# A chunked recurrence: new rows' store and sums' load move from SyncE to GpSimd, and gram blocks are spread by ScalarE

## What is computed

```python
def step(St, inp):
    kt, qt, vt, at, bt = inp
    Sk = jnp.einsum('bhij,bhj->bhi', St, kt)
    err = Sk - vt
    Sn = at[..., None] * St - (bt[..., None] * err)[..., None] * kt[:, :, None, :]
    ot = jnp.einsum('bhij,bhj->bhi', Sn, qt)
    return (Sn, ot)
```

## Time and profile before

| | us |
|---|---|
| median of 3 runs | 3041.19 |
| lowest, highest | 3038.26, 3052.78 |
| the profiled execution | 3051.64 |
| its span | 3050.0 |
| recurrence, first copy at L595 to the last output bank | 681.6 to 1915.7 |

### The profile page before, as it was taken

How to read it: one execution, slowest core, us unless ns; L and a number is a source line. 1 busy time by engine, 2 the same in 40 slices (tenths; PEclk the granted TensorE clock), 3 DMA queues, 4 the chain that set the end, 5 groups by cost and what they waited for, 6 DMA issues and landing times. The chain is left out here.

```text
span 3050.0 us, 41308 instructions
## 1 busy us (share of the span) xinstructions
PE 2080.3 (68%) x12114; PEld 1426.5 (47%) x12114; DVE 1852.3 (61%) x4462; ACT 1056.3 (35%) x2356; POOL 1183.0 (39%) x1443
## 2 busy tenths in 40 slices
PE   8999999966766666556556446599967553479700
PEld 4555555534555554444345335578733331157600
DVE  5777777767776677776667548545537482023234
ACT  2555555534444444444334234222300100112200
POOL 1444444446443333333333323244444217311175
PEclk8999999987787787787777777799989565579955
DMA  3666666663677788999999993422221602048732
GB/s 93 121 121 121 120 121 121 121 148 71 155 189 176 198 210 222 232 243 240 245 241 251 263 281 82 155 76 76 77 83 33 218 11 71 1 144 264 219 101 84
DMA packets 680751, 457.64 MB, mean 150 GB/s; under 512 B 309583, under 2 KB 625790, under 8 KB 674312
## 3 DMA queue, kind: packets, MB, share of 16 engines
q1 hardware_dynamic: 550891, 314.96, 40.9%
q0 software_dynamic: 50080, 96.70, 11.8%
q10 hardware_dynamic: 79616, 44.06, 5.0%
HBM read 245.54 MB, written 207.77 MB: 149 GB/s over the span
## 5 line engine op out<-in xcount | busy, mean ns | idle before, releaser
L918 ACT ACTIVATE p_diag_o<-p_ident,p_gd 128x128 f32<-128x128 f32 x1152 | 361.7, 389 | 509.2 <-PE p_ps_o L874 483.2
L384 DVE SCALAR_TENSOR_TENSOR p_y<-p_ps_proj,p_w,p_y 128x508 f32<-128x508 f32 (+2 forms) x576 | 416.0, 741 | 115.4 <-ACT p_y L298 101.8
L874 PE MATMUL p_ps_o<-p_ws,p_diag_o 128*128 128x128 f32 x1792 | 327.3, 340 | 128.4 <-DVE p_ws L620 80.0
L726 POOL DMA_DIRECT2D p_near_g<-gram x512 | 284.5, 565 | 289.3 <-PE p_ps_n L847 288.8
L874 PEld LDWEIGHTS p_ps_o<-p_ws,p_diag_o 128*128 128x128 f32 x1792 | 284.0, 240 | 200.6 <-DVE p_ws L620 101.8
L833 PE MATMUL p_ps_z<-p_turned,p_gcol 112*32 112x128 f32 x3584 | 159.6, 319 | 318.3 <-DMA p_turned<-history 318.2
L234 PE MATMUL p_ps_proj<-p_x,p_w 128*128 128x512 f32 x768 | 343.1, 597 | 2.7 <-ACT p_beta_t L289 2.7
L198 POOL TENSOR_TENSOR p_kq<-p_y,p_sig 128x512 f32<-128x512 f32 x128 | 162.2, 1271 | 377.6 <-ACT p_sig L309 376.9
L833 PEld LDWEIGHTS p_ps_z<-p_turned,p_gcol 112*32 112x32 f32 x3584 | 104.7, 126 | 382.4 <-DMA p_turned<-history 343.0
L570 DVE SCALAR_TENSOR_TENSOR p_zo<-p_ws,p_gd,p_zo 128x128 f32<-128x128 f32 x768 | 243.9, 351 | 3.8
L564 DVE TENSOR_TENSOR p_ws<-p_ws,p_dec 128x128 f32<-128x128 f32 (+2 forms) x192 | 119.0, 620 | 205.7 <-PE p_ps_o L874 205.7
(11 more groups left out here) (223 smaller groups left out, 3837.0 us busy)
## 6 DMA issues: line engine op xcount, KB each, us to landing
history<-p_hist SPq DMA_DIRECT2D x18, 2048.0 KB, 14.9
gram<-p_gram SPq DMA_DIRECT2D x64, 512.0 KB, 5.4
history_sums<-p_sums ACTq DMA_DIRECT2D x112, 256.0 KB, 5.5
p_zo<-history_sums SPq DMA_DIRECT2D x28, 1024.0 KB, 8.3
p_wgu<-in_wguT SPq DMA_DIRECT2D x64, 352.0 KB
decays<-p_dec SPq DMA_DIRECT2D x64, 256.0 KB, 2.3
beta_v<-p_bv SPq DMA_DIRECT2D x64, 256.0 KB, 2.5
p_dec<-decays POOLq DMA_DIRECT2D x32, 512.0 KB, 6.5
```

The lines of the kernel that those rows point to most:

```text
L384: nc.vector.scalar_tensor_tensor(out=yv[:, :, s:], in0=pv[:, :, 0:T - s], scalar=par[j % 2][:, kind, TAPS - 1 - s:TAPS - s], in1=yv[:, :, ...
L726: pool.dma_start(near_g[h * HALF:(h + 1) * HALF, :, f, h, :], gram_dram[g * BG:(g + 1) * BG, c, c * C:c * C + HALF, h, e0:e0 + HALF] .rear ...
L874: nc.tensor.matmul(ps_o[s // 4 % 2][:, s % 4, :], diag_o[p // DO % NDO][:, p % DO, :], rows[:, r, :], start=(s % 4 == 0 and r == 0), stop= ...
L918: last = nc.scalar.activation(diag_o[n % NDO][:, p % DO, :], ident[:], ACT.Copy, scale=gd[g][:, r, s:s + 1])
```

## The change

- The two stores of a leaf's new rows are issued by GpSimd (`store_u`) right after its wait for leaf_done, ahead of the decays' second half. SyncE waits only for their landing.
- The two loads of the history sums are issued by GpSimd (`load_sums`), for leaf at - 1 in leaf at, behind `load_near(at + 1)` and ahead of the wait for leaf_done.
- `store_o(at)` comes in leaf at, behind leaf_done, in place of the next leaf's beginning.
- `load_near` loads the gram columns compact, 8 DMAs a leaf of 128 rows by 32 values, into part of `near_t` (`near_c`). It waits until near_turn's second half of the leaf before has read near_t (`x_done`), not only for the near products.
- ScalarE (`near_blocks`) makes near_g of it in 16 activations of 128 x 128, each scaled by a column of `own_head`, which is 1 where the partition belongs to head h and 0 elsewhere. It does so behind step 11 (HALF + 3) of the leaf before, and for leaf 0 ahead of everything. near_g is no longer cleared.
- At the start GpSimd issues load_near(0) ahead of the clears and makes own_head; `cleared` comes behind all of it.

```diff
--- before.py
+++ after.py
@@ -437,6 +437,7 @@
     NW = 2
     BANKS = 4
     CHAINS = 4
+    CLEARED = 5 + 2 * NTURN
     UNITS_AFTER = (0, 0, 1, 2, 2, 2, 3, 3)
     UNITS_NEAR = UNITS - sum(UNITS_AFTER)
     with ExitStack() as ctx:
@@ -456,7 +457,9 @@
         diag_o = [m.sb(f"p2_diag_o{i}", [P, DO, P]) for i in range(NDO)]
         near_w = m.sb("p2_near_w", [P, BG, DH])
         near_g = m.sb("p2_near_g", [P, BG, 2, H, HALF])
+        own_head = m.sb("p2_own_head", [P, H])
         near_t = m.sb("p2_near_t", [DH, BG, H, HALF])
+        near_c = near_t[:].rearrange("p b h e -> p (b h e)")[:, 0:BG * 2 * C].rearrange("p (b s) -> p b s", b=BG)
         ps_z = [m.ps(f"p2_ps_z{i}", [P, UB * QUADS, DH]) for i in range(NZ)]
         NN = 2
         ps_n = [m.ps(f"p2_ps_n{i}", [DH, BG // 2, H * HALF]) for i in range(NN)]
@@ -473,7 +476,8 @@
         half_done = m.sem("p2_half_done")
         leaf_done = m.sem("p2_leaf_done")
         near_in = [m.sem(f"p2_near_in{i}") for i in range(2)]
-        near_g_in = m.sem("p2_near_g_in")
+        near_c_in = m.sem("p2_near_c_in")
+        near_g_made = m.sem("p2_near_g_made")
         near_mm = m.sem("p2_near_mm")
         near_cp = m.sem("p2_near_cp")
         x_done = m.sem("p2_x_done")
@@ -718,39 +722,63 @@
             def load_near(at):
 
                 c, g = divmod(at, GR)
-                if at:
-                    pool.wait_ge(near_mm, at * BANKS)
-                for h in range(H):
-                    for f in range(2):
-                        e0 = f * C + HALF
-                        pool.dma_start(near_g[h * HALF:(h + 1) * HALF, :, f, h, :],
-                                       gram_dram[g * BG:(g + 1) * BG, c, c * C:c * C + HALF, h, e0:e0 + HALF]
-                                       .rearrange("b r e -> r b e")).then_inc(near_g_in, DMA)
+                pool.wait_ge(x_done, at * BANKS)
+                for b in range(BG):
+                    pool.dma_start(near_c[:, b, :], gram_dram[g * BG + b, c, c * C:c * C + HALF]
+                                   .rearrange("r h e -> h r e")).then_inc(near_c_in, DMA)
+
+            def load_sums(at):
+
+                c, g = divmod(at, GR)
+                pool.wait_ge(o_out[g], (c + 1) * DMA)
+                if c + 1 < ROUNDS:
+                    pool.wait_ge(kept[g], (c + 1) * 2)
+                for half in range(2):
+                    seqs = slice(half * ZB * H, (half + 1) * ZB * H)
+                    for i in range(NS):
+                        pool.wait_ge(z_out[i], (at * (BG // NS) + (half + 1) * (ZB // NS)) * DMA)
+                    pool.dma_start(zo[g][seqs].rearrange("p f s i -> p (f s) i"), sums_dram[g, seqs]).then_inc(zo_in[g], DMA)
+
+            def store_u(at):
+
+                c, g = divmod(at, GR)
+                for half, rows in ((0, zo[g][:, 0, 1:1 + HALF, :]), (1, w[g][:, 1 + HALF:, :])):
+                    r0 = c * C + half * HALF
+                    pool.dma_start(hist_dram[g, r0:r0 + HALF].rearrange("r p i -> p r i"), rows).then_inc(u_saved[g], DMA)
 
             load_half(0, 0)
             load_gram(0, 0)
             load_half(0, 1)
             load_gram(0, 1)
+            load_near(0)
+            nc.gpsimd.memset(ident[:], 0.0).then_inc(cleared, 1)
+            nc.gpsimd.memset(own_head[:], 1.0).then_inc(cleared, 1)
+            pool.wait_ge(cleared, 2)
+            nc.gpsimd.affine_select(out=ident[:], in_=ident[:], compare_op=ALU.not_equal, fill=1.0, base=0,
+                                    pattern=[[-1, P]], channel_multiplier=1).then_inc(cleared, 1)
+            nc.gpsimd.affine_select(out=own_head[:], in_=own_head[:], compare_op=ALU.is_ge, fill=0.0, base=0,
+                                    pattern=[[-HALF, H]], channel_multiplier=1).then_inc(cleared, 1)
+            pool.wait_ge(cleared, 4)
+            nc.gpsimd.affine_select(out=own_head[:], in_=own_head[:], compare_op=ALU.is_ge, fill=0.0, base=HALF - 1,
+                                    pattern=[[HALF, H]], channel_multiplier=-1).then_inc(cleared, 1)
             for i in range(NTURN):
                 nc.gpsimd.memset(turned[i][:], 0.0).then_inc(cleared, 1)
                 nc.gpsimd.memset(gcol[i][:], 0.0).then_inc(cleared, 1)
-            nc.gpsimd.memset(near_g[:], 0.0).then_inc(cleared, 1)
-            nc.gpsimd.memset(ident[:], 0.0).then_inc(cleared, 1)
-            pool.wait_ge(cleared, 2 * NTURN + 2)
-            nc.gpsimd.affine_select(out=ident[:], in_=ident[:], compare_op=ALU.not_equal, fill=1.0, base=0,
-                                    pattern=[[-1, P]], channel_multiplier=1).then_inc(cleared, 1)
-            pool.wait_ge(cleared, 2 * NTURN + 3)
-            load_near(0)
+            pool.wait_ge(cleared, CLEARED)
             for at in range(LEAVES):
                 c, g = divmod(at, GR)
-                if at:
-                    store_o(at - 1)
                 send_rows(at)
                 if at + 1 < LEAVES:
                     load_half(at + 1, 0)
                     load_near(at + 1)
-                    pool.wait_ge(leaf_done, at + 1)
+                if 0 < at <= ROUNDS * GR:
+                    load_sums(at - 1)
+                pool.wait_ge(leaf_done, at + 1)
+                if c < ROUNDS:
+                    store_u(at)
+                if at + 1 < LEAVES:
                     load_half(at + 1, 1)
+                store_o(at)
                 if c < ROUNDS:
                     pool.wait_ge(u_saved[g], (c + 1) * 2 * DMA)
                     if c + 1 < ROUNDS:
@@ -759,18 +787,15 @@
                     for i in range(2):
                         pool.wait_ge(near_in[i], (at + 1) * ZB * DMA)
                     load_gram(c + 1, g)
-            store_o(LEAVES - 1)
             for g in range(GR):
                 pool.wait_ge(o_out[g], DMA * NCHUNK)
-            for i in range(NS):
-                pool.wait_ge(z_out[i], GR * ROUNDS * (BG // NS) * DMA)
 
         @block.sync
         def _(sp):
             def by_seq(g, r0, n):
                 return hist_dram[g, r0:r0 + n].rearrange("r p i -> p r i")
 
-            sp.wait_ge(cleared, 2 * NTURN + 3)
+            sp.wait_ge(cleared, CLEARED)
             for at in range(ROUNDS * GR):
                 c, g = divmod(at, GR)
                 rows = (c + 1) * C
@@ -797,9 +822,6 @@
                     if c:
                         sp.wait_ge(hist_saved[g], carried(c + 1) * DMA)
                         load_rows(u, 0, known)
-                sp.wait_ge(leaf_done, at + 1)
-                sp.dma_start(by_seq(g, c * C, HALF), zo[g][:, 0, 1:1 + HALF, :]).then_inc(u_saved[g], DMA)
-                sp.dma_start(by_seq(g, c * C + HALF, HALF), w[g][:, 1 + HALF:, :]).then_inc(u_saved[g], DMA)
                 sp.wait_ge(u_saved[g], (c + 1) * 2 * DMA)
                 for u in range(NTURN):
                     if not c:
@@ -808,18 +830,10 @@
                 for u in range(NTURN, UNITS):
                     load_columns(u)
                     load_rows(u, 0, rows)
-                sp.wait_ge(o_out[g], (c + 1) * DMA)
-                if c + 1 < ROUNDS:
-                    sp.wait_ge(kept[g], (c + 1) * 2)
-                for half in range(2):
-                    seqs = slice(half * ZB * H, (half + 1) * ZB * H)
-                    for i in range(NS):
-                        sp.wait_ge(z_out[i], (at * (BG // NS) + (half + 1) * (ZB // NS)) * DMA)
-                    sp.dma_start(zo[g][seqs].rearrange("p f s i -> p (f s) i"), sums_dram[g, seqs]).then_inc(zo_in[g], DMA)
 
         @block.tensor
         def _(pe):
-            pe.wait_ge(cleared, 2 * NTURN + 3)
+            pe.wait_ge(cleared, CLEARED)
 
             def history(at, u):
 
@@ -887,7 +901,7 @@
                     while u < min(units, sum(UNITS_AFTER[:s + 1])):
                         history(at - 1, u)
                         u += 1
-                pe.wait_ge(near_g_in, (at + 1) * 2 * H * DMA)
+                pe.wait_ge(near_g_made, at + 1)
                 near_product(at, 0)
                 near_turn(at, 0)
                 near_product(at, 1)
@@ -900,7 +914,7 @@
 
         @block.scalar
         def _(act):
-            act.wait_ge(cleared, 2 * NTURN + 3)
+            act.wait_ge(cleared, CLEARED)
 
             def diagonals(n):
 
@@ -931,6 +945,16 @@
                 act.dma_start(sums_dram[g, b * H:(b + 1) * H].rearrange("(q h) e i -> (h e) q i", h=4),
                               sums[k % NS][:]).then_inc(z_out[k % NS], DMA)
 
+            def near_blocks(at):
+
+                act.wait_ge(near_c_in, (at + 1) * BG * DMA)
+                if at:
+                    act.wait_ge(near_mm, at * BANKS)
+                own = near_c.rearrange("p b (f s) -> p b f s", f=2)[:, :, :, HALF:]
+                for h in range(H):
+                    last = nc.scalar.activation(near_g[:, :, :, h, :], own, ACT.Copy, scale=own_head[:, h:h + 1])
+                last.then_inc(near_g_made, 1)
+
             def near_rows(at, f):
 
                 if at or f:
```

(3 more changed lines are left out.)

## The result

| | before | after |
|---|---|---|
| median us | 3046.99 (4 runs, 3038.26 to 3054.54) | 2974.73 (4 runs, 2971.49 to 2978.26) |
| ratio, 95% interval | | 0.9764, 0.9739 to 0.9789 |
| profiled execution, its span | 3051.64, 3050.0 | 2975.40, 2973.5 |
| recurrence, first copy to last output bank | 1235.8 | 1172.0 |

Of the 76.5 us between the two spans 63.8 lie in the recurrence, at a granted clock of 0.78 in both.

What follows compares the result with a forecast made beforehand. It took waits in SyncE's order, not DMA work, as the bound. Terms -72 + 1.6 + 1.5 + 8.5 = -60, 10 given back, made -50: 2991 us from a median of 3041.19; own range 2965 to 3012, overall 2965 to 3038.

Steps and rivals of the forecast that it cites:

- the share that I had capped at 0.96 in the rival: Leaves 9 to 13: DMA work is the floor, busy share cannot pass 0.96; 3018 us (3008 to 3032), chance 0.20.
- The rival by which only issues move: SyncE's and GpSimd's loads land no sooner on the same DMA engines; 3052 us, chance 0.10 shared with late sums.
- the signs that I had named for being right: Rows' stores within 1 us of leaf start, first unit at 10, later 12 to 15, leaves 9 to 13 at 73 to 82.
- Rows stored by GpSimd: At leaf_done: two issues of some 0.6 us, then landing; 0.4 us more a leaf in leaves 1 to 4, +1.6 us.
- SyncE freed of the store: Leaves 5 to 10: TensorE's first history unit at about 10 us into the leaf, 26 of 28 us back.
- History stored before the sums: Leaves 11 to 14: store 14 us earlier, 7 added for sharing, first unit 6.7 after landing; about 46 of 60 back.
- I gave back 10 us: Whole recurrence: allowance for transfers that now meet, such as rows' store with history's tail, taking -60 to -50 us.
- The length behind the first unit held fixed: From TensorE's first history unit to leaf end, leaves 5 on: unchanged, 65.7 us in leaf 12, 65.0 in leaf 13.
- Sums loaded by GpSimd: Around leaf_done: land 2 us before to 2 or 3 after, hidden; no cost up to 5 us late.
- Near columns and spreading at nothing: ScalarE's 5.1 us of spreading a leaf: zero cost in leaves 1 to 14 through slack, +1.5 us in leaf 15.
- what the rival feared, ScalarE on the path: Second half of leaves: late near columns make spreading hold the diagonals, 100 us in 11 leaves; 3081 us, chance 0.12.
- The start: Before and in leaf 0: GpSimd's work ahead of `cleared` +3.4 and ScalarE's first spreading 5.1, together +8.5 us.

## Why the prediction was right, and where its steps failed

*What bounds the kernel.* Right that it is a chain of waits through SyncE and no floor of the DMA engines. The whole recurrence, before, in the view that is shown above for after:

```profile
681.60:1917.40 1235.80, 745.37 (x6784) 583.96 (x6784) 849.00 (x2200) 518.28 (x1416) 473.73 (x840) 0.78 0.79 205
```

The same bytes (205 GB/s times 1235.8 us and 217 times 1172.0 are 253 and 254 MB) went through in 63.8 us less, and the share that I had capped at 0.96 in the rival reads 1.01 and 1.02 in leaves 9 to 11. That rival took busy time for capacity, and falls. Whether leaves 9 to 11 of the changed kernel now stand at a higher floor is untested; leaf 12 doesn't, since it takes 77.8 us instead of 86.0 with the outputs last. The rival by which only issues move, named there with the Trainium skill, "DMA: Bandwidth & Descriptors", "Issuing engines are not separate DMA queues", falls too: what moved were waits in SyncE's order, and holding one of them back cost 85 us. Of the signs that I had named for being right, the rows' stores came within 0.8 us of each leaf's start in all 14 leaves, and leaf 0 was as much longer. But from leaf 11 on the first unit came at 16.7 to 27.6 us instead of 12 to 15, and leaves 12 and 13 took 86.0 and 88.2 instead of 73 to 82.

*Rows stored by GpSimd.* The mechanism was right, the wait went from 190.5 to 15.8 us. I forecast +1.6 us in leaves 1 to 4 and got -7.7. The first unit of leaf 1 is 6.1 us later, at 15.8; held loads bring it to 8.3 and the outputs alone, sent last, to 8.4, so it is GpSimd's own traffic behind the store, heads_out above all. The length behind it is shorter in all four.

*SyncE freed of the store.* First unit at about 10 up to leaf 10: measured 8.2 to 13.9 in leaves 2 to 10. Of the forecast 26 us in leaves 5 to 10, 19.6 came as first units and 19.1 more from behind them.

*History stored before the sums: the term that failed.* I forecast 46 us in leaves 11 to 14 and 26.4 came, only 4.7 of them as an earlier first unit. The store did go out 16.7 us earlier into the leaf, 56.5 us instead of the 49 that I had written. Its allowance for meeting other transfers was 7 us; it took 10 (40.0 against 29.8), and it took as long with heads_out sent last or with all of GpSimd's loads held (40.0 and 40.5), so these are not what slows the landing. The known rows of leaf 13 could be loaded 10.4 us into the leaf, against 8 in the forecast. The larger miss is the step after it: 6.7 us from the known rows to the first unit, which took 12.2 before and which I had shortened by the rows' store that drops out of it, took 16.3. So the first unit of leaf 13 came at 26.8 and not at 14 to 15. With heads_out, beta_v and gram held back this step took 9.6 us and the landing came 12.8 us into leaf 13; the first unit of leaf 12 came at 14.7, those of leaves 13 and 14 at 22.4 and 20.7. So the step left out the queue that the freed transfers join: I gave back 10 us for it in the whole recurrence where one late leaf loses that.

*The length behind the first unit held fixed: wrong.* It fell by 54.4 us. I had taken it from two neighbouring leaves of one kernel, which have the same traffic. It isn't a chain of compute alone. What moved out of it are heads_out (issued at the next leaf's first half before), beta_v and gram, which GpSimd had sent once the rows' store had landed, some 22 us into a late leaf and so among the units; in leaf 13 heads_out now goes 5.0 us into the leaf and beta_v 9.3. Putting them back behind the first unit costs 70.9 us of that length. The two errors lie on opposite sides of one sum, the same transfers counted nowhere, so the recurrence fell by 14 us more than forecast and no further off. That is luck: leaves 5 to 14 gave 65 us where I had written 72, but 41 of them came from a length that I had held fixed. And what the total fell beyond the recurrence, 8.5 us of the median, lies in stages in whose code nothing changed.

*Sums loaded by GpSimd.* Right: hidden, 6.3 us of waiting in 8 leaves. That the compact columns carry it I had not said: without them VectorE waits for the sums 9 to 9.5 us a leaf and the move is worth nothing.

*Near columns and spreading at nothing.* As to the size near right, as to slack wrong. The columns land in time (ScalarE waits for them 11.7 us in 8 leaves, 2.4 at most), and VectorE waits at the first step of a leaf only 2.2 us in all. Ahead of the first units of leaves 1 to 14 its wait for own rows rose from 1.1 to 24.1 us, 1.6 a leaf, near the 1.5 that I had forecast; TensorE waits there for history rows anyway, 116.7 us in all. TensorE's wait for diagonals rose from 34.9 to 95.5 us, and of a second set half to two thirds reaches the end: so most of the slack of 5 us is used up, and what the rival feared, ScalarE on the path, begins right behind it. I had priced the columns at nothing; alone they took 11.0 us off the profiled recurrence and 20 off the time, and why is not shown.

*The start.* +8.5 forecast, +9.6 measured, ScalarE's first diagonals at 701.31 behind 4.78 us of spreading. Leaf 15: +1.5 against -0.6, by luck. It takes 56.4 to 58.2 us in the four kernels with the old near loads and 55.8 to 63.9 in the ten with compact columns, and the changed kernel's is the lowest of these, at a granted clock of 0.88 where the others have 0.78 to 0.85.

*What stays open.* The attention output stage, untouched, takes 303.4 to 304.7 us from its first instruction to its last in the four kernels with the old near loads and 298.1 to 300.9 in all ten with compact columns, the one with the small loads put back among them. No run here says where those 5 us come from. How much of the compact columns' 20 us is the DMA engines' work on small packets isn't settled either, as said above. And as leaf 15 shows, a few us of any one profiled recurrence are not its edit's.

## What to carry to other kernels

A wait in the order of a queue that feeds the critical chain can be worth moving even where the DMA engines read nearly full. But don't take its length for the gain (of 190.5 us of waiting 174.7 went, and the recurrence lost 63.8): price the traffic of the queue that takes over, and look at what that queue sends in the next 30 us, since what it sends early is ahead of something. A length that stands still between two neighbouring iterations is not a constant of the kernel, since both have the same transfers in them. Parts of a change may be worth nothing alone and most together (store, sums and columns -13, +3 and -20 us alone, -72 in all, with the outputs' place among it): measure along a path as well as one by one.

## What the hardware showed that I had not expected

- The DMA busy share of a stretch can read above 1 (1.02, 280 to 295 GB/s) and isn't a ceiling at 0.96.
- SyncE is blocked by its own store's issues. The group of three 2 MB history stores held it 15.94 us in the changed kernel's leaf 12 and 24.72 us where the sums' and rows' transfers were under way. These are no waits for VectorE, which was done with its scaling by 1592.03 and 1649.19: of the three issues the first took 0.4 us in both, the others 7.6 and 7.8, and 5.8 and 18.5, and the small load of columns behind them 16.46 and 17.77. So an engine that only issues can be held up at its own stores.
- The spreading's 16 activations with a scale per partition take 4.78 us, 292 ns from start to start.
